# A graph layer and a mixture of experts on one core: VectorE's routing work cut into pieces between step sums, copies of x moved behind the rows

## The reference

```python
h = layernorm(x)
msg = segment_sum(h[src], dst)                 # 100,000 gathered rows
agg = msg / max(degree, 1)
x1 = x + concat([h, agg]) @ W.T + b            # graph layer
xn = layernorm(layernorm(x1)) * gamma + beta
top2 = top_k(xn @ Wr + br, 2); w = softmax(top2)
out = x1 + sum over the 2 chosen of 8 experts of w * (gelu(xn @ W1 + b1) @ W2 + b2)
```

## Time and profile before

| | us |
|---|---|
| median of 3 runs (lowest, highest) | 1796.23 (1794.77, 1799.26) |
| the profiled execution | 1788.75 |
| its span, first to last instruction | 1787.5 |
| TensorE busy | 1241.8 (69%), granted clock 0.842 |
| VectorE / GpSimd / ScalarE busy | 812.6 / 948.0 / 463.2 |

### The profile page before, as it was taken

How to read it: one execution, slowest core, us unless ns; L and a number is a source line. 1 busy time by engine, 2 the same in 40 slices (tenths; PEclk the granted TensorE clock), 3 DMA queues, 4 the chain that set the end, 5 groups by cost and what they waited for, 6 DMA issues and landing times.

```text
span 1787.5 us, 23229 instructions
## 1 busy us (share of the span) xinstructions
PE 1241.8 (69%) x5751; PEld 942.1 (53%) x5751; DVE 812.6 (45%) x2587; ACT 463.2 (26%) x1019; POOL 948.0 (53%) x995
## 2 busy tenths in 40 slices
PE   3223777765874778678787688688788868795881
PEld 2101343442652556556566566566666656684771
DVE  8312663452444445344434444445366565642333
ACT  4200000210220134124124224233322413463440
POOL 3574035666556655655655655665556565115544
PEclk9855998777886889898888889888889889997886
DMA  9732044433333333343333333343344333324553
GB/s 335 247 104 64 1 153 151 133 99 100 110 99 94 107 111 106 115 121 95 113 111 101 110 112 104 109 122 101 115 128 120 105 109 107 101 78 132 160 159 119
DMA packets 128488, 212.63 MB, mean 119 GB/s; under 512 B 25378, under 2 KB 94295, under 8 KB 128119
## 3 DMA queue, kind: packets, MB, share of 16 engines
q0 software_dynamic: 48352, 129.18, 25.2%
q1 hardware_dynamic: 77561, 81.17, 13.7%
q10 hardware_dynamic: 2446, 0.80, 0.2%
HBM read 167.37 MB, written 50.87 MB: 122 GB/s over the span
## 4 chain that ended last, share of the span: by engine, by line
PE 44%; another core or an unknown queue 17%; issue 16%; DVE 11%; ACT 6%; DVEq 2%; DMA 2%; POOL 1%; ACTq 0%; POOLq 0%
PE psum L764 16%; PE psum L833 9%; PE psum L858 8%; DVE acc L1125 5%; PE psum L777 4%; ACT expert_buf L633 2%; PE psum L812 2%; PE psum L778 1%; ACT expert_buf L625 1%; PE psum L845 1%; ACT region L570 1%; DVEq L1118 1%; PE psum L806 1%; PE psum L789 1%
## 5 line engine op out<-in xcount | busy, mean ns | idle before, releaser
L662 POOL DMA_INDIRECT work<-h_rows,srcs x719 | 681.0, 947 | 576.3 <-PE psum L764 324.0
L1125 DVE TENSOR_TENSOR acc<-acc,psum 128x257 f32 x830 | 350.3, 422 | 713.5 <-PE psum L764 329.1
L764 PE MATMUL psum<-work 128*128 128x257 f32 x1438 | 483.6, 450 | 193.7 <-DVE acc L1125 121.9
L764 PEld LDWEIGHTS psum<-work 128*128 128x128 f32 x1438 | 274.7, 219 | 300.3 <-issue 279.1
L833 PE MATMUL psum<-expert_buf 128*128 128x128 f32 x1792 | 235.3, 288 | 40.5 <-ACT expert_buf L625 34.3
L833 PEld LDWEIGHTS psum<-expert_buf 128*128 128x128 f32 x1792 | 230.3, 203 | 50.4 <-ACT expert_buf L625 36.7
L858 PE MATMUL psum<-region,expert_buf 128*128 x896 | 244.7, 422 | 11.6 <-issue 6.5
L633 ACT ACTIVATE expert_buf<-psum,b_col 128x128 f32<-128x128 f32 x448 | 127.8, 370 | 429.7 <-remote 220.0
L858 PEld LDWEIGHTS psum<-region,expert_buf 128*128 128x128 f32 x896 | 186.2, 216 | 49.9 <-issue 21.6
L764 PE MATMUL psum<-region,work 128*128 (+1 forms) x222 | 81.2, 486 | 106.0 <-issue 67.0
L999 DVE TENSOR_TENSOR work<-psum,rel 128x1152 f32<-128x1152 f32 x98 | 126.3, 1289 | 53.6 <-issue 36.7
(11 more groups left out here) (248 smaller groups left out, 896.3 us busy)
## 6 DMA issues: line engine op xcount, KB each, us to landing
expert_buf<-queue SPq DMA_DIRECT2D x112, 128.0 KB
answers<-expert_buf SPq DMA_DIRECT2D x112, 128.0 KB
work<-h_rows,srcs POOLq DMA_INDIRECT x719
region<-in_L_ffn_W_dram SPq DMA_DIRECT2D x16, 512.0 KB
h_rows<-region SPq DMA_DIRECT2D x7, 896.0 KB
own<-h_rows SPq DMA_DIRECT2D x49, 128.0 KB
own<-x_rows SPq DMA_DIRECT2D x49, 128.0 KB
out_dram<-acc SPq DMA_DIRECT2D x49, 128.0 KB
```

The lines of the kernel that those rows point to most:

```text
L662: pool.indirect_dma_start(place_of(g)[:, 0:D], None, h_rows, bass.IndirectOffsetOnAxis(srcs[:, cell_of:cell_of + 1], 0)).then_inc(got[g % ...
L764: summed.up(pe.matmul(STEP_BANKS[t % BANKS][:, 0:GW], hot[:, k, :], rows, start=True, stop=True))
L1125: added.up(dve.tensor_tensor(sums, sums, STEP_BANKS[t % BANKS][:, 0:GW], ALU.add))
```

## The change

On VectorE the three routing functions and `results_rows` are cut at places where nothing was in flight, and the pieces are put at different t, each behind the step sum of that t:

- `route_choice` keeps L1006 to L1011 at CHOICE; the rest is `route_picks`, at CHOICE + 1. TensorE's ranks stay at CHOICE + 2.
- `route_places` becomes `route_ranks` (shares, ranks, sum over them, carry) at CHOICE + 4, and `route_places` at CHOICE + 5, which was CHOICE + 3. The scatters keep their t: their distance to PLACES is now 15, not 17.
- `tile_list` becomes five pieces, at PLACES + 1, + 3, + 5, + 7 and + 9; the last raises `list_up`. `LISTS` is PLACES + 9, and the stores of padding on SyncE that follow it move by 10 steps.
- `results_rows` becomes `find_blocks`, `find_shifts`, `result_rows` at three t in a row, every fourth t for the first 39 tiles (every third before), so that 9 of them fall after step 829, and every third for the last ten (every one before).

When the expert tiles begin (`begin_at`) comes out the same for all 112, and so do `y_at` and `BACK`.

In the head, all seven `copy_x` are issued after all of `h_rows` has landed. ScalarE takes the root of group b + 1 after the fifth tile of group b. VectorE's statistics of group 1 move behind the edge tables (after L956), and the scales of group 0 come right after `less`.

```diff
-    PLACES = [t + 3 for t in CHOICE]
-    LISTS = [t + 1 for t in PLACES]
-    SCATTER = [t + AHEAD + 2 for t in PLACES]
+    RANKED = [t + 4 for t in CHOICE]
+    PLACES = [t + 1 for t in RANKED]
+    LISTS = [t + 9 for t in PLACES]
+    SCATTER = [t + AHEAD for t in PLACES]
...
+    FOUND = [LISTS[FLUSH] + 4 + 4 * r for r in range(CUT)]
+    FOUND += [max(FOUND[-1], LISTS[NB - 1]) + 4 + 3 * r for r in range(NT - CUT)]
...
         for b in range(NLB):
             h_up.wait(sp, b)
             sp.dma_start(h_rows[...], xall[...]).then_inc(s_hst, 16)
-            for c in COPIED[b]:
-                copy_x(c)
+        sp.wait_ge(s_hst, 16 * NLB)
+        for c in range(NLB):
+            copy_x(c)
...
-    COPIED = [[0], [1, 2], [3], [], [], [], [4, 5, 6]]
...
+        roots(0)
         for b in range(NLB):
-            ln_var.wait(act, b)
-            ln_sd.up(act.activation(sd[:, b, :], sd[:, b, :], ACT.Sqrt))
             ln_up.wait(act, b)
             for t in range(b * LB, (b + 1) * LB):
                 i = act.activation(xall[:, t, :], ...)
+                if t == b * LB + ROOT_AT and b + 1 < NLB:
+                    roots(b + 1)
...
         less_up.up(...)
-        tile_stats(1)
-        tile_scales(1)
+        tile_scales(0)
         ranked.wait(dve)
...
-        tile_stats(2, scales=False)
-        tile_scales(2)
+        tile_stats(1, scales=False)
+        tile_scales(1)
         placed.wait(dve, 0)
...
-        for b in range(3, NLB):
-            tile_stats(b, scales=(b > 3))
+        for b in range(2, NLB):
+            tile_stats(b, scales=(b > 2))
...
         dif_up.up(dve.tensor_tensor(dif[:, 0:n], top[:, 0:n, 1], top[:, 0:n, 0], ALU.subtract))
+
+    def route_picks(b):
...
-                if t == PLACES[b]:
-                    route_places(b)
-                if t == LISTS[b]:
-                    tile_list(b)
+                if t == CHOICE[b] + 1:
+                    route_picks(b)
+                if t == RANKED[b]:
+                    route_ranks(b)
+                if t == PLACES[b]:
+                    route_places(b)
+                if t == LISTS[b] - 8:
+                    list_avail(b)
+                if t == LISTS[b] - 6:
+                    list_experts(b)
+                if t == LISTS[b] - 4:
+                    list_tiles(b)
+                if t == LISTS[b] - 2:
+                    list_rows(b)
+                if t == LISTS[b]:
+                    list_served(b)
             for r in range(NT):
-                if t == (LISTS[FLUSH] + 2 + 3 * r if r < CUT else LISTS[NB - 1] + 1 + r - CUT):
-                    results_rows(r)
+                if t == FOUND[r] - 2:
+                    find_blocks(r)
+                if t == FOUND[r] - 1:
+                    find_shifts(r)
+                if t == FOUND[r]:
+                    result_rows(r)
```

More of the change, by code:

```diff
@@ L59, in build @@
     LB = 7
+    ROOT_AT = 4
     NLB = NT // LB
@@ L391, in build @@
     END = BACK[-1] + 10
+    FOUND = [LISTS[FLUSH] + 4 + 4 * r for r in range(CUT)]
+    FOUND += [max(FOUND[-1], LISTS[NB - 1]) + 4 + 3 * r for r in range(NT - CUT)]
+    assert all(f < b for f, b in zip(FOUND, BACK))
     def begins(t):
@@ L573, in scalar_head, with roots @@
         acc_zero.up(act.copy(acc[:, CLEARED:NT, :], zcol[:, 0:1].unsqueeze(1).broadcast_to([P, NT - CLEARED, GW])))
+    def roots(b):
+        ln_var.wait(act, b)
+        ln_sd.up(act.activation(sd[:, b, :], sd[:, b, :], ACT.Sqrt))
     def scalar_stream():
@@ L1036, in route_places @@
         d_own.then(dve.tensor_reduce(place[:, :, lo:hi], prod[:, :, 0:n, :], AX_X, ALU.add))
+        rank_cp.wait(dve, b)
+        d_own.then(dve.tensor_tensor(carry[:, :], carry[:, :], total[:, :], ALU.add))
+    def route_places(b):
+        lo, hi = BATCHES[b]
+        n = hi - lo
         d_own.then(dve.tensor_tensor(place[:, :, lo:hi], place[:, :, lo:hi], valid[:, lo:hi].unsqueeze(1).broadcast_to([P, 2, n]), ALU.mult))
@@ L1042, in route_places, with list_avail @@
         d_own.then(dve.tensor_scalar(block_i[:, :, 0:n], place_i[:, b % 2, :, 0:n], P.bit_length() - 1, None, ALU.arith_shift_right))
-        dve.tensor_copy(block[:, :, lo:hi], block_i[:, :, 0:n])
-        d_own.then(dve.tensor_tensor(carry[:, :], carry[:, :], total[:, :], ALU.add))
-    def tile_list(b):
-        n, first, last = UPTO[b + 1] - UPTO[b], LISTED[b], b == NB - 1
+        d_own.then(dve.tensor_copy(block[:, :, lo:hi], block_i[:, :, 0:n]))
+    def list_avail(b):
         if b in (FLUSH, NB - 2):
@@ L1056, in tile_list, with list_experts @@
         d_own.then(dve.tensor_tensor(avail[:, :], cnt[:, :], served[:, 0:X], ALU.subtract))
+    def list_experts(b):
+        n, first = UPTO[b + 1] - UPTO[b], LISTED[b]
         dve.tensor_scalar(jtile[:, 0:n], iota[:, 0:n], served[:, 0:1], None, ALU.add)
@@ L1062, in tile_list, with list_tiles @@
                                      cum[:, :].unsqueeze(1).broadcast_to([P, n, X]), ALU.is_ge))
-        dve.tensor_reduce(eq_[:, first:first + n], ge[:, 0:n, :], AX_X, ALU.add)
+        d_own.then(dve.tensor_reduce(eq_[:, first:first + n], ge[:, 0:n, :], AX_X, ALU.add))
+    def list_tiles(b):
+        n, first = UPTO[b + 1] - UPTO[b], LISTED[b]
         d_own.then(dve.tensor_tensor(gt[:, 0:n, :], ge[:, 0:n, :], steer[:, :].unsqueeze(1).broadcast_to([P, n, X]), ALU.mult))
@@ L1068, in tile_list, with list_rows, list_served @@
         d_own.then(dve.tensor_tensor(jtile[:, 0:n], jtile[:, 0:n], live[:, 0:n], ALU.mult))
+    def list_rows(b):
+        n, first = UPTO[b + 1] - UPTO[b], LISTED[b]
         d_own.up(dve.scalar_tensor_tensor(off_i[:, first:first + n], eq_[:, first:first + n], float(QUEUE), jtile[:, 0:n], ALU.mult, ALU.add))
[L1070 to L1071 removed]
+        d_own.up(dve.tensor_scalar(ew_i[:, first:first + n], eq_[:, first:first + n], float(X - 1), None, ALU.min))
+        d_own.then(dve.tensor_scalar(shift[:, first:first + n], iota[:, 0:n], float(P), float((UPTO[b] - (FIRST_TILES if b > FLUSH else 0)) * P), ALU.mult, ALU.add))
         dve.tensor_scalar(tile_block[:, first:first + n], off_i[:, first:first + n], 1.0 / P, None, ALU.mult)
[L1073 to L1075 removed]
+        d_own.then(dve.tensor_tensor(shift[:, first:first + n], shift[:, first:first + n], off_i[:, first:first + n], ALU.subtract))
+    def list_served(b):
+        n = UPTO[b + 1] - UPTO[b]
+        if b < NB - 1:
             d_own.then(dve.tensor_tensor(cum[:, :], avail[:, :], cum[:, :], ALU.subtract))
@@ L1080, in tile_list, with cells_of, find_blocks, find_shifts @@
         if b == FLUSH:
-            d_own.up(dve.scalar_tensor_tensor(carry[:, :], cnt[:, :], float(P), qbase[:, :], ALU.mult, ALU.add))
-        d_own.settle()
-        list_up.up(dve.memset(zcol[:, 0:1], 0.0))
-    def results_rows(r):
-        cells = slice(0, LISTED[FLUSH + 1]) if r < CUT else slice(LISTED[FLUSH + 1], QT)
-        for s in range(2):
-            i = dve.scalar_tensor_tensor(hit[:, s, cells], tile_block[:, cells], block[:, s, r:r + 1], shift[:, cells], ALU.is_equal, ALU.mult)
-        d_own.then(i)
-        d_own.then(dve.tensor_reduce(found[:, :], hit[:, :, cells], AX_X, ALU.add))
+            d_own.then(dve.scalar_tensor_tensor(carry[:, :], cnt[:, :], float(P), qbase[:, :], ALU.mult, ALU.add))
+        list_up.up(dve.memset(zcol[:, 0:1], 0.0))
+    def cells_of(r):
+        return slice(0, LISTED[FLUSH + 1]) if r < CUT else slice(LISTED[FLUSH + 1], QT)
+    def find_blocks(r):
+        for s in range(2):
+            d_own.up(dve.scalar_tensor_tensor(hit[:, s, cells_of(r)], tile_block[:, cells_of(r)], block[:, s, r:r + 1], shift[:, cells_of(r)], ALU.is_equal, ALU.mult))
+    def find_shifts(r):
+        d_own.settle()
+        d_own.up(dve.tensor_reduce(found[:, :], hit[:, :, cells_of(r)], AX_X, ALU.add))
+    def result_rows(r):
+        d_own.settle()
         answer_up.up(dve.tensor_tensor(answer_i[:, :, r], place[:, :, r], found[:, :], ALU.add))
```

11 lines of the change are left out of this document (4 added, 7 removed).

## The result

The kernel after takes 1823.7 us (median of 3 runs, 1819.6 to 1823.9) where before took 1796.2: a ratio of 1.0143, 95% interval 1.0113 to 1.0173. It is slower by 27.5 us; the forecast was 33 us less. Measured again with ten runs it was 1.0098 (1.0063 to 1.0133). The profiled execution has a span of 1822.6 us, 35.1 more than before's 1787.5.

The account below looks back on a forecast made before the run. No engine is full; the time was taken as TensorE's work plus its pauses, about 60 us of them from routing. Terms -22 - 9 + 3 - 5 = -33 took 1796.2 to 1763 us; own range 1745 to 1785.

Parts of the forecast that it names:

- Scatters, 0: GpSimd's scatters: places come two steps later, it waits about 3.6 us longer per batch, no gather comes late; 0 us.
- Lists, -22 us: VectorE's list burst of 4.7 us, cut into five pieces, no longer makes TensorE pause; -22 us, bounds 0 and -26.3.
- Clock behind the gaps, -9 us: TensorE's granted clock no longer drops behind list pauses over 3 us; 2.3 us in four windows, bounds 0 and 23.
- a few us in sum: Sign of being right: TensorE's pauses in ten windows from LISTS - 8 total a few us, where they were 26.3.
- Choice, +3: TensorE's rank matmuls at CHOICE + 2 wait one step sum, 0.63 us, longer in five batches; +3 us, bounds 0 and 7.6.
- places, 0: VectorE's places burst, cut in two, stays covered by TensorE's own work (30.03 of 30.11 us); 0 us.
- Searches, 0: VectorE's searches, some 1 us each, now in three pieces, add no wait; 0 us.
- Head, -5 us: First gather, at 59.6 us, goes earlier as copies no longer queue before the last rows' store; -5 us, bounds 0 and 10.
- Slower, through GpSimd: Rival: GpSimd waits at SCATTER, then issues back to back longer; one 5.2 us stall in nine batches, 1810 us; chance 0.15.
- Nothing comes of it: Rival: TensorE's late results leave VectorE behind, pieces delay sums as the burst did; only the head's gain stays, 1791; chance 0.13.

Follow-up runs that it names:

- places_later_2: Kernel before with only the places moved 2 steps later, scatters at their steps, so 15 behind the places; 1.0108 of before on a chip of 1790 us.
- the second pair: Profiles of the kernels before and after, both run again unchanged on chips of 1790 us; after measured 1.0098 of before.
- head_only: Kernel before with only the head of after (copies, roots, order of statistics and scales); 1.0025 on the chip of 1426 us, 0.9967 on one of 1790 us.
- before_again: Kernel before, unchanged, run again against itself for its profile on a chip of 1790 us; 0.9956 of before.
- scatter_later_2: Kernel after with scatters 2 steps later, 17 behind the places as in before; 1.0029 of before on a chip of 1790 us.

## Why the prediction was wrong

Two steps failed, and both were needed for the sign: with the lists' -31 us (clock included) after would have been faster even so, and with the scatters at 0 it would have been about the same.

- *Scatters, 0.* It said that GpSimd "will wait about 3.6 us longer per batch" and that this costs nothing, since it runs 17 steps ahead and "no gather comes late". The wait was nearly right: 26.7 us more at the first scatters of nine batches, 3.0 each. And no step in the steady part waited for its gather, as far as the trace names the waits. The cover was the wrong one: I asked who waits for the gathers and not what the steps lose while GpSimd makes up for its standing. Measured +20 us (`places_later_2`). A reading was wrong beside it: of the 57.7 us that GpSimd "already waits there", 53.0 are three waits of the last batches (15.0, 16.5 and 21.5 us, from 1514 us on), and in the nine batches among the steps it was 4.7 us in all. So the wait was nearly new there, not a longer one.
- *Lists, -22 us.* The burst's step fell by 28.7 us in eight batches, and it was given back in the next seven steps. Measured 0 to +6 us, of -31 with the clock. The lower bound, "0 if another wait fills every gap", was the case. "It is the burst that makes the gap" was read from who was busy in the window; it doesn't say what would bound the steps next.
- *Clock behind the gaps, -9 us.* TensorE's busy time rose by 13.4 us instead (9.1 in the second pair), and the pauses did not go but moved and grew. In ten windows over the pieces of after (the step before LISTS - 8 to LISTS) it stands 106.9 us, in 9 steps each, where "a few us in sum" was the sign of being right:

```profile
sum 234.73, PE 127.81 PEld 92.21 DVE 106.21 ACT 27.11 POOL 146.09; mean PE 12.78 PEld 9.22 DVE 10.62 ACT 2.71 POOL 14.61
```

- *Choice, +3, and places, 0.* Open. The wait at the ranks rose by 1.2 us in the first pair and by 9.3 in the second; the bound was 7.6. What it costs no run tells apart. *Searches, 0*: not tried alone.
- *Head, -5 us.* Right on the chips of 1790 us: 0.9967 is 6 us, and the trace of after has the first gather at 53.88 for 59.72:

```profile
46.86 2.06 ACT L575 ACTIVATE region<-region,pay 128x256 f32<-128x256 f32 x4
...
53.63 4.58 SPq L495 DMA_DIRECT2D x_rows<-in_x_dram  x7
53.88 0.96 POOL L673 DMA_INDIRECT region<-h_rows,srcs  x1 [13.71 <-DMA h_rows<-region]
```

  The first sum came 7.1 us earlier (63.0 for 70.1 us). What the copies do beside the gathers was wrong, and that the head gained even so was luck in part. The prediction gave such a gather 0.7 us by the round-robin of the page "DMA: Bandwidth & Descriptors", section "Queues, rings and completion order", of the Trainium skill; the traces of this case do not show such a share: the gathers behind the copies took 10.3 to 18.7 us to land (`head_only`), and in after the steps 0, 2, 4 and 6 are summed at 63.0, 66.6, 70.4 and 76.2 us. This looks more like the order of issue. The first gather, issued at 53.88, had one copy of the seven before it, and that may be why its step was early. On the chips of 1790 us the steps behind it were slow in before too (step 9 at 94.1 us, in after at 82.4), so the copies cost nothing; on the chip of 1426 us they cost what the head gave.

Measured terms: -6 (head), 0 to +6 (lists), +20 (places), together +14 to +20, and after is 17 us over before in the larger comparison, 27.5 in the first. That the sum fits does not prove its parts, since giving the scatters their distance back returned 10 us and not 20. The rival *Slower, through GpSimd* (1810 us, chance 0.15) had the engine and the wait. It asked for 3.7 us per batch and got 3.0. Its sum was luck in part: it put 47 us on a forecast whose gain of 33 did not come. It also looked for the loss at CHOICE + 20 to + 32, where the scatters stand in the program; GpSimd runs 17 steps ahead, and the loss lies in the steps CHOICE to + 15, while the fifteen behind them got shorter. *Nothing comes of it* was right for the lists. A sign stood in rows that the prediction quotes: 183.6 us of late results, and the steps of the head at 5.6 us while GpSimd issues. I took both as a background that the change doesn't touch.

Open: why TensorE's results come late beside GpSimd's issues on some chips; by what way the standing costs time, as the late results in all are no longer in `places_later_2` than in `before_again` (185.9 and 186.2 us from 240 to 1590), though they are in the fifteen steps behind the choices (60.9 and 37.1 in eight batches); and the 13 to 15 us that `scatter_later_2` keeps.

## What to carry to other kernels

When a producer of GpSimd's data is moved later, count what GpSimd stands, per batch, as a cost (here 20 us for 24 of standing), unless the engine has real pauses behind that place in which it can catch up; a lead of gathers covers the gathers only. A gap filled by one engine's burst is a gain only if the trace shows that nothing else bounds those steps: compare how many steps pass in the neighbouring stretch, not only who is busy in the gap. When a time in a schedule is moved, print everything that is derived from it: here the scatters' step also sets when the expert tiles begin. And look at the longest unbroken stretch of issues whose results nobody needs yet.

## What was not expected of the hardware

The same program took 1426 us on one chip and 1790 us on the others, with nearly the same busy time of GpSimd and VectorE. Waits with no releaser on the core were there on the slower ones alone; the largest single difference stands in the head, where 41 gathers in 50 us left TensorE 18 matmuls on one chip and 132 on the other. Two pauses of GpSimd of 2.1 and 2.6 us, and shorter ones behind them, were enough for the results to come at their normal pace again. The gathers issued just behind the copies of x, from another engine's queue, took 10.3 to 18.7 us to land, against 2.8 in the steps. And `before_again` differed from before by 0.44% with an interval that excludes 1.
